# States 4 to 7 of units 1 to 3 by TensorE, from diagonals that transfers spread; pair 5 of C to GpSimd; half of a weight's scaling one unit earlier

## The reference, cut to what matters

```
x = x + tanh(g_x) * mamba(ctx, layernorm(x))         # z is the normed x
x = x + tanh(g_f) * ffn(layernorm(x))
mamba: u  = silu(conv(ctx @ w_in.T) + b)             # 4 batches, 512 channels, 512 times
       dt, B, C from projections of u                # 16 states
       h[n,t] = h[n,t-1] * exp(dt[t] * A[n]) + dt[t]*u[t] * B[n,t]
       y[t]   = sum over n of h[n,t] * C[n,t];  y = (y + D*u) * silu(z)
ffn:   ternary weights (|w| mean as scale), activations rounded to 8 bits,
       silu(gate) * up, then down
```

## Time and profile before

| | |
|---|---|
| median of 3 runs | 612.04 us (611.45 to 612.93) |
| profiled execution, its time | 611.89 us |
| its span | 609.9 us |
| mean granted TensorE clock | 0.966 |
| busy: VectorE, GpSimd, TensorE, ScalarE | 556.6, 521.0, 516.7, 507.7 us |

### The profile page before, as it was taken

How to read it: one execution, slowest core, us unless ns; L and a number is a source line. 1 busy time by engine, 2 the same in 40 slices (tenths; PEclk the granted TensorE clock), 3 DMA queues, 4 the chain that set the end, 5 groups by cost and what they waited for, 6 DMA issues and landing times. The chain is left out here.

```text
span 609.9 us, 9603 instructions
## 1 busy us (share of the span) xinstructions
PE 516.7 (85%) x3190; PEld 359.8 (59%) x3190; DVE 556.6 (91%) x766; ACT 507.7 (83%) x776; POOL 521.0 (85%) x298
## 2 busy tenths in 40 slices
PE   6999676768675888989879898989789999998997
PEld 2443265747564676767656767675667575764443
DVE  1899989999999899999899999998999999988774
ACT  3879788986999789899978898998798989777773
POOL 1558799999999899999999899999998999973340
PEclk9999859778799999999999999999999999999999
DMA  8992951530661010115521111145411110000323
GB/s 273 403 412 108 325 197 34 192 136 1 240 243 53 0 53 2 35 34 208 203 93 35 34 37 36 35 157 223 121 35 35 36 36 18 1 18 21 84 53 86
DMA packets 38866, 66.32 MB, mean 109 GB/s; under 512 B 12177, under 2 KB 20369, under 8 KB 36002
## 3 DMA queue, kind: packets, MB, share of 16 engines
q1 hardware_dynamic: 38818, 65.72, 30.9%
HBM read 55.49 MB, written 8.13 MB: 104 GB/s over the span
## 5 line engine op out<-in xcount | busy, mean ns | idle before, releaser
L889 POOL TENSOR_TENSOR area_s<-area_s,b_bc 128x1024 f32<-128x1024 f32 x117 | 275.2, 2364 | 14.1 <-DVE u_all L1510 9.9
L515 PE MATMUL pY<-ident,area_s 128*128 128x128 f32 x532 | 87.9, 291 | 54.5 <-DVE area_s L1518 54.5
L584 PE MATMUL pG<-wq_gu,area_f 128*128 128x512 fp8e4 x448 | 108.0, 380 | 4.2 <-ACT area_f L1106 2.9
L1510 DVE TENSOR_TENSOR_SCAN area_s<-pA,area_s 128x512 f32<-128x512 f32 x88 | 105.1, 1205 | 5.1 <-ACT pA L1169 5.1
L515 PEld LDWEIGHTS pY<-ident,area_s 128*128 128x128 f32 x532 | 62.2, 146 | 75.4 <-DVE area_s L1518 67.9
L1169 ACT ACTIVATE pA<-dt_all,a_neg 128x512 f32<-128x512 f32 x145 | 97.7, 682 | 10.7 <-DVE area_s L1510 5.9
L881 POOL TENSOR_TENSOR u_all<-u_all 128x1024 f32<-128x1024 f32 x44 | 103.9, 2361 | 0.2 <-DMA u_all<-bc_rows 0.2
L1518 DVE TENSOR_TENSOR area_s<-area_s,pC 128x512 f32<-128x512 f32 x132 | 87.0, 661 | 0.9 <-DVE area_s L1510 0.8
L509 PE MATMUL pC<-ident,xdT 128*128 128x128 f32 x528 | 84.2, 288 | 3.2 <-DVE area_s L1518 2.0
L584 PEld LDWEIGHTS pG<-wq_gu,area_f 128*128 128x128 bf16 x448 | 41.6, 98 | 48.9 <-ACT area_f L1106 5.2
L509 PEld LDWEIGHTS pC<-ident,xdT 128*128 128x128 f32 x528 | 65.4, 146 | 8.1 <-DVE area_s L1518 6.6
(11 more groups left out here) (218 smaller groups left out, 1123.0 us busy)
## 6 DMA issues: line engine op xcount, KB each, us to landing
b_bc<-bc_rows SPq DMA_DIRECT2D x14, 1024.0 KB, 6.7
area_s<-x SPq DMA_DIRECT2D x32, 256.0 KB, 2.9
u_all<-bc_rows SPq DMA_DIRECT2D x14, 512.0 KB, 6.5
b_bc<-w_gate SPq DMA_DIRECT2D x1, 4096.0 KB, 14.0
dt_all<-x SPq DMA_DIRECT2D x1, 4096.0 KB, 24.3
area_f<-w_up SPq DMA_DIRECT2D x1, 4096.0 KB, 33.6
area_f<-w_down SPq DMA_DIRECT2D x1, 4096.0 KB, 14.9
out<-area_f SPq DMA_DIRECT2D x16, 256.0 KB, 2.1
```

Source lines behind the costliest of these rows:

```text
L515: mm = pe.matmul(pY[:, k * P:(k + 1) * P], src[:, k * P:(k + 1) * P], ident[:, :], is_transpose=True, start=(first and k == 0), stop=(last ...
L584: mm = pe.matmul(bank, xqT[t % 2][:, k, :], wq_gu[:, k, m, c * GW:(c + 1) * GW], start=(k == 0), stop=(k == NT - 1))
L889: gp.tensor_tensor(db[c % NDB], du[s % 2].rearrange("p (a l) -> p a l", a=1).to_broadcast([P, CH, L]), b_bc[:, CH * c:CH * c + CH, :], ALU ...
L1510: dve.tensor_tensor_scan(h, at, dbu, 0.0, ALU.mult, ALU.add).then_inc(S["s_scan"], 1)
```

## The change

- In units 1 to 3, `dt*u*B` of pairs 2 and 3 (states 4 to 7) is made by TensorE (`pe_pairs`). GpSimd has two `times_b` less in each of them, and three products with C in place of two (`pooled`): pairs 1, 3 and 5.
- The diagonals of these four states are made by transfers: GpSimd zeroes a tile, SyncE stores it four times into a DRAM tensor `b_spread` (1 MB), then writes the 512 elements of each state's B row on the diagonals there by a transfer with single elements (`spread_first`), and later loads the whole into `b_bc` (`load_diagonals`).
- `du_transpose` and `copy_duT` run for units 1 to 3 at steps 14 and 15 of the unit before. `db_state` stands at steps 1 to 4.
- `w_total(2)` moves from step 12 to 10, `w_means(2)` from 14 to 11; two of the four `w_scale(2, ..)` move from unit 3 to steps 13 and 15 of unit 2.
- The SBUF area kept for GpSimd's own descriptors shrinks to 4096 bytes a partition; no transfer here is issued by GpSimd.

```
 def pooled(s):
-    return (1, 3) if s < PLAIN else (0, 2, 4, 6)
+    if s == 0:
+        return (1, 3)
+    return (1, 3, 5) if s < PLAIN else (0, 2, 4, 6)
+def pe_pairs(s):
+    if 0 < s < PLAIN:
+        return (2, 3)
+    return (PE_PAIR,) if s >= PE_FROM else ()
 def pool_pairs(s):
-    return [c for c in range(NCH) if s < PE_FROM or c != PE_PAIR]
+    return [c for c in range(NCH) if c not in pe_pairs(s)]
...
             def load_b(b, quarters=range(4)):
                 for q in quarters:
-                    if b:
+                    if b == 1 and q == 1:
+                        sp.wait_ge(S["s_dbp"], DBP_AT[NT])
+                    elif b:
...
+            def spread_first():
+                sp.wait_ge(S["k_zero"], 1)
+                sp.dma_start(b_spread.rearrange("j (p f) -> p j f", p=P),
+                             zeros[:, :].rearrange("p (a f) -> p a f", a=1).to_broadcast([P, NSPREAD, L])).then_inc(S["c_zero"], 16)
+                sp.wait_ge(S["c_zero"], 16)
+                for j in range(NSPREAD):
+                    spots = b_spread[j].rearrange("(k r) -> k r", k=NT)[:, 0:P * P:P + 1]
+                    sp.dma_start(spots, bc_rows[0, CH * PE_PAIR + j].rearrange("(k p) -> k p", k=NT),
+                                 allow_slow_non_contiguous=True).then_inc(S["c_spread"], 16)
+            def load_diagonals():
+                sp.wait_ge(S["c_spread"], 16 * NSPREAD)
+                sp.wait_ge(S["s_dbu"], db_count(0, 3))
+                first = CH * PE_PAIR
+                sp.dma_start(b_bc[:, first:first + NSPREAD, :].rearrange("p j (k l) -> p (j k) l", k=NT),
+                             b_spread.rearrange("j (k p l) -> p (j k) l", k=NT, p=P)).then_inc(S["d_spread"], 16)
...
             for b in range(1, BATCH):
                 sp.wait_ge(S[f"c_bst{b}"], 16)
+            spread_first()
             load_z(2)
             load_z(3)
             load_x(2)
+            load_diagonals()
             load_u(2)
...
             def db_state(s, i):
                 n = CH * PE_PAIR + i
+                pe.wait_ge(S["s_duT"], DUT_AT[s] + 1)
+                if s < PLAIN:
+                    pe.wait_ge(S["d_spread"], 16)
+                    pe.wait_ge(S["s_scan"], s * NS + n - 3)
...
+                    if n == 2 and s:
+                        db_state(s, 1)
                     if n - 1 in own(s):
                         y_sum(s, n - 1)
+                    if n == 1 and s:
+                        db_state(s, 0)
+                    if n in (3, 4) and s:
+                        db_state(s, n - 1)
+                    for j, pair in enumerate(pooled(s)):
+                        if n == CH * pair + 5:
+                            y_sum_pooled(s, j)
                     if n == 10:
                         y_skip(s)
+                    if n == 14 and s + 1 < PLAIN:
+                        du_transpose(s + 1)
...
-                    if s == 2 and n == 12:
+                    if s == 2 and n == 10:
                         pe.wait_ge(S["s_szT"], s + 1)
                         w_total(2)
...
                     if n == 8:
                         dt_u(s + 1)
+                        if s:
+                            times_c(s, 2)
...
-                    if s == 3 and n % 2 == 0 and n < 2 * NW:
-                        w_scale(2, n // 2)
-                    if s == 3 and n in (8, 10, 12):
-                        w_sign(2, 7 - n // 2)
+                    if s == 2 and n in (13, 15):
+                        w_scale(2, n // 2 - 6)
+                    if s == 3 and n in (1, 3):
+                        w_scale(2, n // 2 + 2)
+                    if s == 3 and n in (5, 7, 10):
+                        w_sign(2, 5 - n // 2 if n < 10 else 1)
+                    if n == 15 and s + 1 < PLAIN:
+                        copy_duT(s + 1)
...
-                    if s == 2 and n == 14:
+                    if s == 2 and n == 11:
                         w_means(2)
```

More of the change, by code:

```diff
@@ L48, in pooled, with pe_states @@
 def pooled(s):
-    return (1, 3) if s < PLAIN else (0, 2, 4, 6)
+    if s == 0:
[5 more added lines that the diff above has]
+    return (PE_PAIR,) if s >= PE_FROM else ()
+def pe_states(s):
+    return [CH * c + i for c in pe_pairs(s) for i in range(CH)]
 PE_FROM = PLAIN + 1
 PE_PAIR = 2
+NSPREAD = 4
 ALONE = 11
@@ L96, in by_pe @@
 def by_pe(s, n):
-    return s >= PE_FROM and n // CH == PE_PAIR
+    return n // CH in pe_pairs(s)
+DUT_AT = [sum(bool(pe_pairs(i)) for i in range(s)) for s in range(UNITS + 1)]
+DBP_AT = [sum(len(pe_states(i)) for i in range(s)) for s in range(UNITS + 1)]
 VE, RR, M2, REC1, XS, SS, RH, M3, REC2, FAC, MH, XSUM, DEV = range(13)
@@ L133, in build @@
 def build(nc, x, ctxT, g_x, g_f, w_in, w_conv, b_conv, w_xp, w_dt, b_dt, a_log, d_skip, w_gate, w_up, w_down,
-          bc_rows, u_rows, out):
+          bc_rows, u_rows, b_spread, out):
     with ExitStack() as stack:
@@ L155, in build @@
         diag_d = sb("diag_d", [P, P])
+        zeros = sb("zeros", [P, L])
         neg_half = sb("neg_half", [P, UNITS])
@@ L207, in build @@
         duT = carve(area_s, 8192, L).rearrange("p (k d) -> p k d", k=NT)
-        diag_b = [b_bc[:, CH * PE_PAIR + i, :].rearrange("p (k l) -> p k l", k=NT) for i in range(CH)]
+        diag_b = [b_bc[:, CH * PE_PAIR + i, :].rearrange("p (k l) -> p k l", k=NT) for i in range(NSPREAD)]
         xz = [carve(area_s, 8704 + L * i, L) for i in range(2)]
@@ L303, in load_c @@
             def load_c(b):
-                for j, pair in enumerate(pooled(NT * b)):
+                for j, pair in enumerate(pooled(max(NT * b, 1))):
                     if b and j < len(pooled(NT * b - 1)):
@@ L549, in du_transpose @@
                 pe.wait_ge(S["s_szT"], s)
+                if s == 3:
+                    pe.wait_ge(S["k_wm"], 7)
                 for k in range(NT):
@@ L626, in down @@
                     if z_done < UNITS:
-                        pe.wait_ge(S["s_duT"], z_done - PE_FROM + 1)
+                        pe.wait_ge(S["s_duT"], DUT_AT[z_done] + 1)
                     else:
@@ L641, in keep_on @@
                 else:
-                    pe.wait_ge(S["s_duT"], s - PE_FROM + 1)
+                    pe.wait_ge(S["s_duT"], DUT_AT[s] + 1)
                 for k in range(NT):
@@ L827, in _ @@
             gp.memset(neg_half[:, :], -0.5).then_inc(S["k_const"], 1)
+            gp.memset(zeros[:, :], 0.0).then_inc(S["k_zero"], 1)
             gp.wait_ge(S["k_const"], 9)
@@ L1160, in exponential @@
                 if by_pe(s, n):
-                    act.wait_ge(S["s_scan"], (s - 1) * NS + CH * (PE_PAIR + NDB) + CH)
-                    act.activation(db[PE_PAIR][:, n % CH, :], dt_all[:, s, :], ACT.Exp, scale=a_neg[:, s % NT, n:n + 1]).then_inc(S["s_exp"], 1)
+                    act.wait_ge(S["s_scan"], (s - 1) * NS + CH * (n // CH + NDB) + CH)
+                    act.activation(db[n // CH][:, n % CH, :], dt_all[:, s, :], ACT.Exp, scale=a_neg[:, s % NT, n:n + 1]).then_inc(S["s_exp"], 1)
                     return
@@ L1188, in copy_duT @@
             def copy_duT(s):
-                act.wait_ge(S["s_dup"], s - PE_FROM + 1)
-                past(act, S["s_dbp"], CH * (s - PE_FROM))
+                act.wait_ge(S["s_dup"], DUT_AT[s] + 1)
+                past(act, S["s_dbp"], DBP_AT[s])
                 act.activation(duT.rearrange("p k d -> p (k d)"), pT[:, :], ACT.Copy).then_inc(S["s_duT"], 1)
@@ L1197, in diagonal @@
                 else:
[L1198 removed]
+                    act.wait_ge(S["s_dbp"], DBP_AT[b * NT - 1] + i + 1)
                 n = CH * PE_PAIR + i
@@ L1649 @@
     u_rows = nc.dram_tensor("u_rows", (UNITS, P, L), F32, kind="Internal").ap()
+    b_spread = nc.dram_tensor("b_spread", (NSPREAD, NT * P * P), F32, kind="Internal").ap()
     out = nc.dram_tensor("out", _OUT, F32, kind="ExternalOutput").ap()
-    build(nc, *aps, bc_rows, u_rows, out)
+    build(nc, *aps, bc_rows, u_rows, b_spread, out)
     r = run_bass_kernel_spmd(nc, [arrays], core_ids=[0])
```

20 lines of the change are left out of this document (8 added, 12 removed).

## The result

The changed kernel takes 622.16 us (median of 4 runs, 622.14 to 622.39), the kernel before 611.75 us (median of 4, 610.54 to 612.93). The ratio is 1.0171, with an interval of 1.0151 to 1.0192: 1.7% slower. The forecast was 621.6 us. The profiled execution took 622.16 us too, its span is 620.4 us against 609.9 before.

The account below looks back on a forecast made before the run. It took VectorE to bound units 1 to 3, GpSimd right behind. Unit 1 +7.6, unit 2 -0.6, units 3 and 4 +2.55, together +9.5 us, gave 621.6 us, 1.6% slower, range 614 to 634.

Parts of the forecast that it names:

- The stall of unit 1: Unit 1: TensorE waits for the late diagonals, then runs at half clock; VectorE stalls 9.2 us, unit net +7.6 us.
- median landing of like loads: Unit 1: the diagonals' load lands 6.9 us after its issue, the median between 4.3 and 14.2 us, at 110.4.
- Unit 2: +0.35 for late gated_y, -1.16 for moved products, -0.4 for a gap gone, +0.6 for the mean: -0.6 us.
- the mean's, +0.6: Unit 2: w_total behind y_sum and y_skip takes 1.75 us against 1.14 before w_means wants it, +0.6 us.
- Units 3 and 4: +0.35 us for late gated_y and +2.2 us for GpSimd's late residual(3), unit 3's saving lost: +2.55 us.
- its lower end, at 0.8 us: Unit 3 with the head of unit 4: the least loss, 0.8 us, if only x_rstd(0) is late.
- The sum: Whole kernel: the units together +9.5 us on the profiled execution, 611.89 to 621.4 us, nothing changed after x_scales(0).
- the clock to stay up: Units 2 and 3, steps 1 to 4: db_state is hidden, 0.89 us each at full clock, if the clock stays up.
- Rival 1: Before unit 1: the spread's single-element transfers end late, adding 0 to +32 us to the stall; chance 0.27.
- Rival 2: Unit 1 and residual(3): diagonals land in time and GpSimd catches up, 3.7 us less, 608.4 us; chance 0.04.
- Rival 3: Unit 1: full clock and early landing shorten the stall, residual(3) costs its lower end, 613 to 616 us; chance 0.13.
- 3.5 us less work on VectorE: Units 1 to 3: two products less on VectorE in each, 1.16 us a unit, 3.5 us together.

Follow-up runs that it names:

- e1: The changed kernel with the load of the diagonals issued ahead of the z and x loads, nothing else: 614.65 us, ratio 1.0058 to the kernel before.
- e2: The changed kernel, load still late, with twelve groups of four idle transposes on TensorE before the first db_state of unit 1: 618.65 us.
- e3: The changed kernel, load still late, with GpSimd's residual(3) ahead of times_b(4, 4) in unit 4: 624.03 us.
- e4: e3 with GpSimd's x_rstd(0) also moved ahead of times_b(4, 5): 620.34 us.
- e8: e1 with pair 5 of C left to VectorE in unit 3 only: 610.54 us, ratio 0.9985 to the kernel before.
- e7: e1 with pair 5 of C left to VectorE in units 1 to 3: 612.18 us, ratio 1.0012 to the kernel before.
- e10: e6 with two groups of four idle transposes on TensorE at step 10 of units 1 to 3: 608.85 us, ratio 0.9944 to the kernel before.
- e9: e6 with pair 5 of C left to VectorE in unit 3: 609.39 us, ratio 0.9955 to the kernel before.
- e11: e6 with x_rstd(1) moved ahead of dt_u(5) and times_b(5, 0) in unit 4: 610.85 us, ratio 0.9982 to the kernel before.
- e6: e4 with the load early as in e1, w_total(2) ahead of y_skip, y_sum_pooled(s, 2) ahead of the last-but-one y_sum: 609.32 us.

## Why the prediction was right

**The stall of unit 1.** Predicted +9.2 - 1.16 - 0.46 = +7.6 us, measured +7.2. The steps held one by one: the x load at 103.0 (102.81), the diagonals behind it landing in 6.9 us (6.7), TensorE at half clock afterwards (0.50). The stall itself was 8.27 us and not 9.2: the product of state 4 starts at 116.69 and not at 117.6. The load landed 0.3 us sooner, and TensorE's work from there to that product took some 6.5 us where 7.1 were put down for half clock throughout; the granted clock had risen again by 115.6, so that the third `db_state` (eight in 1.54 us) and what follows were partly at full. e1 shows the queue's order as the cause; e2 splits it into about 5.7 us of landing and 2.5 of clock. That the median landing of like loads was the right one to take was in part luck: of 4.3 to 14.2 us it came at 6.7, and in e3 the same late load took 8.2.

**Unit 2.** Predicted -0.6, measured +0.75. The saving is there. `gated_y` came 0.27 us late, predicted 0.35. The term that was mis-sized is the mean's, +0.6, which was worked out at full clock alone: there the wait was 0.63 us in five runs (e1 to e4 and e8), but in the changed kernel's profile TensorE was at half in that place and it was 1.90.

**Units 3 and 4.** Predicted +0.35 + 2.2 = +2.55, measured -0.71 + 2.66 = +1.95. GpSimd's 2.3 us came through, 1.31 us before `stats(0)` and 1.18 us behind ScalarE before the reduction. But the text laid all of it on `residual(3)`; e3 shows that moving this alone changes nothing, and e4 that GpSimd's whole work up to `x_rstd(0)` binds as well. The prediction had that path only as its lower end, at 0.8 us; in e3, where it binds by itself, it costs 2.31 us behind 1.12 us for ScalarE. The 1.24 us before the product of state 12 in unit 3 had no term: it is once more `y_skip` at half clock.

**The sum.** Predicted +9.5 us on the profiled execution, measured +10.3 us (622.16 against 611.89), of which 9.7 us up to `x_scales(0)`. An overestimate in unit 1 and one in units 3 and 4 (0.4 and 0.6 us) hid an underestimate of 1.35 us in unit 2, and the tail's 0.7 us had no term. The total is closer than its parts, which is luck. Where the prediction needed the clock to stay up, at steps 1 to 4 of units 2 and 3, it did: it stood at 1.00 from 134.15 to 144 and from 161.69 to 171, and no gap arose there. What it left out is that the clock falls later in these units, at `y_skip`, with a price on VectorE.

**The rivals.** Rival 1 (a late spread) did not come about. Rival 2 needed a landing 3.6 us after the issue; it was 6.7. Rival 3 needed full clock behind the wait, and e2 shows what that would have given: 618.65 us, more than its 613 to 616, since it wants an early landing too. e7, which has TensorE's added matmuls and takes the time of the kernel before, speaks against these as a cause, though its profile has gaps of 0.22 and 0.55 us behind them in unit 2.

**What was expected and is real.** 3.5 us less work on VectorE was true, and was lost in four places: a load in the wrong place of SyncE's order, GpSimd's work just before unit 4, the waits for the matmuls placed later, and the clock. Mending the first three and shortening the fourth gives e10, 2.8 us below the kernel before. That is not four fifths of the 3.5 us, as the stages show. Units 1 and 2 take 49.60 us in e10 against 52.95 before, 3.35 us less, most of it 2.3 us of moved work and 0.84 us of gaps that the kernel before had of its own (0.46 and 0.38). Units 3 and 4 take 60.24 against 60.38, so the 1.16 us of unit 3 bring next to nothing; e9, which leaves them on VectorE, is 2.6 us below the kernel before too.

## What to carry to other kernels

A load that is written down behind another inherits that one's wait. When a new load goes into a queue whose order is written by hand, look at what the entry before it waits for; here 7.5 us hung on the place of one line. When work goes from the engine that bounds to the one right behind it, count the receiving engine's whole work up to its next deadline, and not only in the units where the work is added. And where TensorE has idle stretches (it is busy 62 to 76% of units 1 to 3 here), the instruction that decides may run at either of two speeds: price it at both.

## What the runs showed of the hardware

**Single elements are not as dear as feared.** Page of the changed kernel for the window 88.6 to 93.4, in which the four transfers of L362 run:

```profile
DMA  1112238311112333312113233422222344545794
DMA packets 2080, 0.07 MB, mean 15 GB/s; under 512 B 2056, under 2 KB 2056, under 8 KB 2079
```

2048 elements of 4 bytes, from DRAM to DRAM, took 4.8 us from the first packet to the last, or 7.9 us in e1 from the first issue to the moment at which SyncE's wait for them ended. The 2056 small packets bear out the rule of the Trainium skill ("DMA: Bandwidth & Descriptors", "Rules for kernel authors") that a strided last dimension becomes one descriptor per element. Its other rule, that an outermost dimension of four keeps a transfer to four engines, fits the busy share of mostly 1 to 3 tenths of 16 engines, but is not shown by it. If four engines did it, an element took 9.4 ns of one (4.8 us / 512), less than half of the 21.7 ns that rival 1 was priced with.

**One instruction has two durations, and that decides where the gaps lie.** The eight matmuls of `y_skip` take 1.06 us at the upper level, 1.92 at the lower and 1.48 to 1.65 where the level changed among them (e4, e11). One of the slower kinds left VectorE 0.83 to 1.31 us idle before the product of state 12, or 1.90 us before the mean. Which unit's is hit differs from version to version (unit 1 in e1, units 2 and 3 in the changed kernel, units 1 and 3 in e6), so an edit of a microsecond could only be judged with the clock's rows beside it. Eight idle transposes ahead of `y_skip` kept it at 1.00 in unit 1 (e10). In e2 the granted clock stood at 0.50 from 104.2 to 107.2 although TensorE, after 1.99 us of idling, had been busy without a break since 102.78; from 108.2 on it was 1.00. So the idle work did not hold the level there, but TensorE was at full clock by the time the load landed.
